# Mamba phase of a four-block network: each scan step cut into two halves, the next chunk's preparation placed by half steps, mean square and row scaling on ScalarE, and GpSimd's product released by the next step's scan

## The reference, cut to what matters

```
n      = rmsnorm(x) * norm_w
xb, z  = split(n @ in_w.T)
xb     = silu(causal_conv(xb, 4 taps) + cb)
dt, B, C = split(xb @ xp_w.T)                  # 16 + 16 + 16
delta  = softplus(dt @ dtw.T + dtb)
dA     = exp(delta[..., None] * -exp(a_log))
mi     = delta[..., None] * B * xb[..., None]
v      = 0.6 * v + mi                          # over the tokens
h      = dA * h + v                            # over the tokens
y      = sum_n h[..., n] * C[..., n] + dp * xb
x      = x + (y * silu(z)) @ out_w.T
```

## Time and profile before

| | |
|---|---|
| median of 3 runs | 5011.13 us |
| lowest, highest | 5005.98, 5019.97 us |
| the profiled execution's own time | 5015.33 us |
| its span | 5013.6 us |
| mean granted clock of TensorE | 0.856 of full speed |
| busy share PE, DVE, ACT, POOL | 74%, 61%, 39%, 41% |

### The profile page before, as it was taken

The page is one execution under the profiler, slowest core; times in us unless marked ns, Lnnn a source line. Parts: engine busy times, 40 slices in busy tenths (PEclk is TensorE's granted clock), DMA queues, the critical chain, the costliest instruction groups (busy, mean ns, idle before and its releaser), DMA issues. The chain is left out here.

```text
span 5013.6 us, 95420 instructions
## 1 busy us (share of the span) xinstructions
PE 3692.2 (74%) x29740; PEld 2429.9 (48%) x29741; DVE 3059.5 (61%) x5150; ACT 1968.5 (39%) x4502; POOL 2051.2 (41%) x1225
## 2 busy tenths in 40 slices
PE   6888879368878878888567888878787431888870
PEld 3555556245545555455345555455554231666660
DVE  3444423457787877878557777877787651333334
ACT  1121112155555655556255555555555120323320
POOL 1011000145565656656445665656556505000006
PEclk8887879779988999899779889989999755999995
DMA  1000000112121221212121121211212152000003
GB/s 44 0 0 0 0 18 0 50 36 67 44 68 45 54 59 46 66 45 64 37 52 52 45 68 45 65 46 47 67 45 67 59 200 83 30 29 30 30 24 100
DMA packets 156167, 241.78 MB, mean 48 GB/s; under 512 B 26450, under 2 KB 84082, under 8 KB 153076
## 3 DMA queue, kind: packets, MB, share of 16 engines
q1 hardware_dynamic: 146164, 210.61, 14.9%
q0 software_dynamic: 9600, 26.23, 1.6%
HBM read 118.86 MB, written 36.18 MB: 31 GB/s over the span
## 5 line engine op out<-in xcount | busy, mean ns | idle before, releaser
L870 POOL TENSOR_TENSOR m_hc<-m_h,m_Cb 128x1024 f32<-128x1024 f32 x512 | 1216.9, 2380 | 1061.5 <-PE m_bank L1244 534.6
L998 DVE TENSOR_TENSOR_SCAN m_h<-m_dA,m_hlast,m_bank 128x256 f32<-128x256 f32 x2048 | 1338.4, 724 | 174.1 <-PE m_bank L1262 167.8
L1244 PE MATMUL m_bank<-m_hc,ident 128*128 128x512 f32 x2048 | 1166.9, 698 | 42.4 <-POOL m_hc L870 37.4
L1260 PE MATMUL m_bank<-m_M,m_U 128*128 128x64 bf16 x8192 | 650.1, 199 | 461.4 <-DVE m_h L998 279.0
L1260 PEld LDWEIGHTS m_bank<-m_M,m_U 128*128 128x128 bf16 x8192 | 585.0, 102 | 679.8 <-DVE m_h L998 486.3
L1115 ACT ACTIVATE m_dA<-m_delta,m_rate 128x256 f32<-128x256 f32 x2048 | 872.1, 503 | 38.2 <-DVE m_h L998 34.7
L1262 PE MATMUL m_bank<-m_M,m_U 112*128 112x64 bf16 x8192 | 649.2, 199 | 0.0
L1262 PEld LDWEIGHTS m_bank<-m_M,m_U 112*128 112x128 bf16 x8192 | 582.6, 102 | 69.6 <-issue 61.7
L1244 PEld LDWEIGHTS m_bank<-m_hc,ident 128*128 128x128 f32 x2048 | 397.7, 216 | 357.3 <-issue 301.1
L947 DVE SCALAR_TENSOR_TENSOR m_cv<-m_xpre,m_conv,m_cv 128x256 f32<-128x256 f32 x384 | 312.9, 856 | 19.5 <-ACT m_cv L1054 15.0
L1121 ACT COPY m_hlast<-m_h 128x4 f32<-128x4 f32 x512 | 97.9, 191 | 507.2 <-DVE m_h L998 506.8
(11 more groups left out here) (264 smaller groups left out, 5975.0 us busy)
## 6 DMA issues: line engine op xcount, KB each, us to landing
m_Cb<-m_c_rows SPq DMA_DIRECT2D x256, 256.0 KB, 3.2
m_M<-m_Mhi SPq DMA_DIRECT2D x128, 256.0 KB, 4.5
m_M<-m_Mlo SPq DMA_DIRECT2D x64, 256.0 KB, 4.9
m_U<-m_Uhi SPq DMA_DIRECT2D x128, 128.0 KB, 2.9
g_stage<-in_e_w SPq DMA_DIRECT2D x16, 1024.0 KB, 6.9
slots_x<-x_res SPq DMA_DIRECT2D x36, 256.0 KB, 6.3
x_x_in<-slots_x SPq DMA_DIRECT2D x72, 128.0 KB, 2.0
slots_y<-x_y POOLq DMA_DIRECT2D x72, 128.0 KB, 2.0
```

Source lines behind the costliest of these rows:

```text
L870: nc.gpsimd.tensor_tensor(hc[:, n % 2], h[:, n % RING], Cb[:, g % 2, n % NG, :].unsqueeze(1).broadcast_to([P, KI, CM]), ALU.mult).then_inc ...
L998: nc.vector.tensor_tensor_scan(h[:, n % RING, m, :], dA[:, n % RING, m, :], VB[(n % 2) * 2 + m // 2][:, (m % 2) * CM:(m % 2 + 1) * CM], hl ...
L1244: last = nc.tensor.matmul(Y[half][:], net.ident[:], hc[:, n % 2, 2 * half:2 * half + 2, :], start=(n == 0), stop=(n == NS - 1))
L1260: nc.tensor.matmul(bank[:, at:at + SUB], U1[:, par, j, m * P:(m + 1) * P], M1[:, par, j, n, :], start=True, stop=False)
```

## The change

`OFF` becomes 8 and counts half steps; the index `at` of a head now runs over half steps, so a chunk's step n has the halves 2n and 2n + 1, and the head of chunk c+1 has index half + 8. Velocity, accumulate, decays and scan are cut in two: each half g takes the channel groups 2g and 2g + 1. The order on PE within a half is velocity g, accumulate g, then the pieces.

The pieces move to these head indices (local half steps in brackets; those from 24 on are in the chunk before): squares 0 (24) and root 1 (25), row scaling 3 (27), transposes 4 (28), xT 5 (29), halo 6 (30), in_proj one tile at each of 6 to 13 (30, 31, 0 to 5), ACT's copies 8 and 10 (0, 2), convolution 11 and 13 (3, 5), silu 15 (7), x_proj 16 (8), B rows 18 (10), dt projection 20 (12), Gf and first Mf 20, second Mf 22, first Mlo 24 (16), second Mlo and Glo 26 (18), series 25 (17), softplus end 27 (19), u 28 (20), transposes of u 30 (22), Uhi 31 (23), Ulo 32 (24), carry matmuls 33 (25), chi 34 (26), clo 35 (27). The tail: gate at half 4, POOL's multiplication at half 6, out_proj at 9 and 10 (now into H1), addition to x at 11. x_proj and the B rows now use H0.

The statistics on DVE (bn_stats, bn_aggr and two small tensor_tensors) are replaced by two ACTIVATEs of Square with an accumulator on ACT, and the row scaling is done by two ACTIVATEs on ACT. `product` waits for one more scan: the first quarter of the next step's. On POOL the product of step 15 moves to step 0 of the next chunk. On SP, place_m now stands ahead of spread 6.

The core of the diff:

```diff
-RING, LEAD, OFF, NG = 4, 2, 5, 2
+RING, LEAD, OFF, NG = 4, 2, 8, 2
...
-                    for g in (4, 5, 6):
+                    for g in (4, 5):
                         spread(c, par, g)
                     if not last:
                         place_m(c + 1, 1 - par)
+                    spread(c, par, 6)
+                    if not last:
                         place_u(c + 1, 1 - par)
...
-                    if at == 15:
-                        matrix_low(q, 1)
-
-                def tail(t, par, slot):
-                    if slot == 2:
+                def tail(t, par, at):
+                    if at == 6:
                         pool.wait_ge(s["gate_done"], 1 + t * KI + KI)
...
-                def product(c, par, n):
+                def product(c, par, n, next_scan=1):
                     k = c * NS + n
                     g = n // NG
-                    pool.wait_ge(s["scan_done"], 1 + AHEAD + (k + 1) * KI)
+                    pool.wait_ge(s["scan_done"], 1 + AHEAD + (k + 1) * KI + next_scan)
                     pool.wait_ge(s["acc_done"], 1 + AHEAD + k - 1)
...
+                    tiles = [xm[:, (q + 1) * TM + j, :] for j in range(TM)]
+                    if at == 0:
+                        for j in range(TM):
+                            nc.scalar.activation(xr[:, j, :], tiles[j], ACT.Square, accum_out=ssq[:, j:j + 1]
+                                                 ).then_inc(s["rms_in"], 1)
+                    if at == 3:
+                        act.wait_ge(s["rms_out"], 1 + q + 1)
+                        act.sem_inc(net.carrier, 1)
+                        for j in range(TM):
+                            nc.scalar.activation(xr[:, j, :], tiles[j], ACT.Copy, scale=rstd[:, j:j + 1]
+                                                 ).then_inc(s["xr_done"], 1)
...
                 def slots(c, par, more, more2):
                     for n in range(NS):
-                        if n < NS - 1:
-                            velocity(c, par, n + 1)
-                        elif more:
-                            velocity(c + 1, 1 - par, 0)
-                        if n >= 2:
-                            accumulate(c, n - 2)
-                        else:
-                            late(c, n)
-                        tail(c, 1 - par, n, more)
-                        if more:
-                            head(c + 1, 1 - par, n + OFF)
-                        if more2 and n + OFF >= NS:
-                            head(c + 2, par, n + OFF - NS)
...
+                        for at in (2 * n, 2 * n + 1):
+                            g = at % 2
+                            if n < NS - 1:
+                                velocity(c, par, n + 1, g)
+                            elif more:
+                                velocity(c + 1, 1 - par, 0, g)
+                            if n < 2:
+                                late(c, n, g)
+                            elif n > 2:
+                                accumulate(c, n - 2, g)
+                            elif g == 1:
+                                accumulate(c, 0, 0)
+                                accumulate(c, 0, 1)
+                            tail(c, 1 - par, at, more)
+                            if more:
+                                head(c + 1, 1 - par, at + OFF)
+                            if more2 and at + OFF >= 2 * NS:
+                                head(c + 2, par, at + OFF - 2 * NS)
```

More of the change, by code:

```diff
@@ L928, in head @@
                 def head(q, par, at):
[L929 to L942, removed]
+                    if at in (11, 13):
+                        g = (at - 11) // 2
                         dve.wait_ge(s["pre_done"], 1 + q * 2 + g + 1)
-                        dve.wait_ge(s["halo_done"], 1 + q + 1)
                         for k in range(TAPS - 1):
@@ L1238, in accumulate, with tail @@
-                def accumulate(c, n):
+                def tail(t, par, at, more):
+                    if at in (9, 10):
+                        j = at - 9
+                        if j == 0:
+                            pe.wait_ge(s["gated_done"], 1 + t + 1)
+                            pe.wait_ge(s["xm_done"], 1 + t)
+                            if more:
+                                pe.wait_ge(s["z_done"], 1 + (t + 1) * 2 + 2)
+                        for k in range(KI):
+                            last = nc.tensor.matmul(H1[:, j * D:(j + 1) * D], u[:, k, j * P:(j + 1) * P],
+                                                    w_out[:, k, :], start=(k == 0), stop=(k == KI - 1))
+                        if j == TM - 1:
+                            last.then_inc(s["out_psum"], 1)
@@ L1239, in accumulate @@
+                def accumulate(c, n, half):
                     k = c * NS + n
-                    pe.wait_ge(s["hc_done"], 1 + AHEAD + k + 1)
+                    if half == 0:
+                        pe.wait_ge(s["hc_done"], 1 + AHEAD + k + 1)
                     if n == 0:
-                        pe.wait_ge(s["gate_done"], 1 + c * KI + KI)
-                    for half in range(2):
-                        last = nc.tensor.matmul(Y[half][:], net.ident[:], hc[:, n % 2, 2 * half:2 * half + 2, :],
-                                                start=(n == 0), stop=(n == NS - 1))
@@ L1246, in accumulate, with velocity @@
-                    last.then_inc(s["acc_done"], 1)
-                def velocity(c, par, n):
+                        pe.wait_ge(s["gate_done"], 1 + c * KI + 2 * half + 2)
+                    last = nc.tensor.matmul(Y[half][:], net.ident[:], hc[:, n % 2, 2 * half:2 * half + 2, :],
+                                            start=(n == 0), stop=(n == NS - 1))
+                    if half == 1:
+                        last.then_inc(s["acc_done"], 1)
+                def velocity(c, par, n, g):
@@ new lines, in velocity @@
+                    bank = VB[(n % 2) * 2 + g]
+                    for m in (2 * g, 2 * g + 1):
+                        for j in range(NSUB):
+                            at = (m % 2) * CM + j * SUB
+                            nc.tensor.matmul(bank[:, at:at + SUB], U1[:, par, j, m * P:(m + 1) * P],
+                                             M1[:, par, j, n, :], start=True, stop=False)
+                            last = nc.tensor.matmul(bank[:, at:at + SUB], U2[:, par, j, m * P:(m + 1) * P],
+                                                    M2[:, par, j, n, :], start=False, stop=True)
@@ L1266, in slots, with late @@
+                    last.then_inc(s["v_psum"], 1)
+                def late(c, n, half):
+                    if not (isinstance(c, int) and c == 0):
+                        accumulate(c - 1, n + NS - 2, half)
                 def slots(c, par, more, more2):
                     for n in range(NS):
-                        if n < NS - 1:
-                            velocity(c, par, n + 1)
-                        elif more:
-                            velocity(c + 1, 1 - par, 0)
-                        if n >= 2:
-                            accumulate(c, n - 2)
-                        else:
-                            late(c, n)
@@ L1287, in _ @@
+                for at in range(2 * NS + OFF):
                     head(0, 0, at)
```

270 lines of the change are left out of this document (133 added, 137 removed).

## The result

The changed kernel takes 4887.3 us (median of four executions, 4877.3 to 4896.9) against 5014.0 for the kernel before in the same session: 0.9748 of it, interval 0.9724 to 0.9773, which is 127 us less. The direction and the range of the prediction held; its size did not, since 54 us were forecast. The profiled execution took 4885.9 us, with a span of 4884.2.

The account below looks back on a forecast made before the run. Waits, not a full engine, bound the kernel: a chain forecast at 44.4 + 25.4 + 3.8 + 12.9 = 86.5 us per period against 88.3. 30 x 1.8 = 54 us less gives 4961, by the median 4957; range 4865 to 5080.

Parts of the forecast that it names:

- The chain: One period of the Mamba loop, velocity 0 to velocity 0, as pieces A, B, C: 86.5 us forecast against 88.3.
- The sum is 88.3.: Present period of one chunk: pieces of 44.15, 25.4 and 18.7 us, cut at velocity 0 at 2033.73 and 2122.05.
- Product 5 starts at 44.4: End of the stretch from velocity 0 to GpSimd's product 5, forecast at 44.4 us; 44.15 before.
- piece A: From velocity 0 to GpSimd's product 5, with TensorE and VectorE handing over: 44.15 us before, 44.4 forecast.
- I take 25.4 again: GpSimd's twelve instructions from product 5, reordered with two lock waits kept: 25.4 us, so u ends at 69.8.
- piece B: GpSimd's nearly packed stretch of twelve instructions from product 5: 25.4 us before and in the forecast.
- u to transposes, Uhi and Ulo takes 3.8 us: Start of piece C: from u's end at 69.8 to Ulo done at 73.6, 3.8 us.
- the last piece: Piece C, SP's DMAs and the carries up to the next velocity 0: 18.7 us before, 3.8 + 12.9 forecast.
- The prologue and the last chunk of a layer keep their order: zero.: Edges outside the 30 periods, forecast to change by zero.
- Occupancy pays in full: Rival: VectorE's relief shows in full, at least 4.5 us per period, 135 us in all: 4875; chance 0.18.
- Release is no release: Rival: a later scan changes nothing for GpSimd's product; period within 0.5 us of 88.3, 5011 within 15; chance 0.14.
- One lock wait too many: Rival, pieces A and B: each whole-product wait of 2.35 us lengthens the period; one gives 5027, two 5098; chance 0.28.

Follow-up runs that it names:

- e2_rms: The kernel before, with only the mean square and the row scaling moved to ScalarE: 5001.1 us, 0.9974 of the kernel before.
- e3_both: The kernel before, with second Mlo ahead of u, M's DMAs ahead of spread 6, and mean square and rows on ScalarE: 4927.3 us, 0.9831 of it.
- e9_whole_gate5: The changed kernel with TensorE's velocity and accumulate in whole steps and GpSimd's gate multiplication ahead of product 2: 4686.4 us, 0.9331 of the kernel before.
- e4_norel: The changed kernel with the product released by its own scan again, as before: 4870.0 us, 0.9720 of the kernel before.
- e6_whole: The changed kernel with TensorE issuing both halves of velocity and accumulate at a step's first half, other engines keeping halves: 4794.9 us, 0.9576 of the kernel before.
- e1_order: The kernel before, with only the second Mlo moved ahead of u and M's DMAs ahead of spread 6: 4934.0 us, 0.9839 of the kernel before.
- e7_gate5: The changed kernel with GpSimd's gate multiplication one half step earlier, ahead of product 2: 4803.9 us, 0.9578 of the kernel before.

## Why the prediction was right and wrong

**The chain was right.** Counted from velocity 0 at 1987.11, forecast against this period: gate multiplication starts 25.9 against 25.3; xb ends 31.8 against 31.1; x_proj 3.45 against 3.53; product 5 starts 44.4 against 43.4; u ends 69.8 against 68.35; Ulo ends 73.6 against 71.1; carries issued 78.6 to 79.3 against 77.15; velocity 0 again 86.5 against 84.6. Of the signs that the text named, these are there: U's DMAs behind u (2.8 us, some 4 forecast), M issued at product 9, z not before 28 us (29.06), x_proj's idle time (4.60) and its lower clock. Three are not as named: the period is 84.6 and not 86 to 87, TensorE's wait for the carries is still there but 2.7 us a time and not 4 to 5, and a convolution instruction takes 624 ns in the mean and not below 600.

**The size was missed by several terms, nearly all to one side.** The steps that failed:
- "The sum is 88.3." The base period came from one pair of velocity 0. Eleven periods in the middle of a layer give 88.74 in the mean. 30 x 0.44 is 13 us. (From clo to clo all 30 periods have a mean of 88.29, since the first and the last of a layer are shorter; those became shorter in the changed kernel too, so middle periods are to be compared with middle periods.)
- "Product 5 starts at 44.4", piece A: 43.4, and about 41.7 in the periods in which TensorE does not show its lower level behind velocity 0. Thirteen periods of the changed kernel give 84.9 in the mean, with 82.7 to 87.6 between single ones.
- "I take 25.4 again", piece B: 24.95. As foreseen, the lock waits changed place and stayed two: products of 3.33 and 3.35 us instead of the long Mf and Mlo.
- "u to transposes, Uhi and Ulo takes 3.8 us": 2.77. The 3.8 came from a place where an accumulate stood in the way: it ran to 2100.26, 1.37 us past the end of u. In the last piece Ulo to clo took 6.0 us against the 4.9 (by clo) or 5.7 (by the queue) of the forecast, and clo to velocity 0 7.47 against some 7.9; the two together are 13.47, which is 0.57 more than the 12.9 of the sum and goes against the other three.
- "The prologue and the last chunk of a layer keep their order: zero." The edges changed too. From clo to clo, the 15 periods of the first layer lost 55.6 us and those of the second 60.0; the stretch between the layers lost 7.7 (170.0 to 162.3), and that before the first clo 2.7. So 10 us lay in a term that I had set at zero without a row.

Together: a period 1.6 us shorter than forecast is 48, the base 13, the edges 10, and with the 54 forecast that makes 125 of the 127. Counted directly, the 30 periods lost 115.6 us from clo to clo, 3.85 each, where 1.8 each was forecast. No one of the terms is large; the forecast was short by more than half because its own gain, 1.8 of 88.3 us, was a small difference of large terms.

**The costs set at nothing.** Mean square and rows were costed at zero. Done alone they are worth 15 us at most (e2_rms) and 7 beside the order (e3_both): right. The accumulating form that no row showed takes 0.41 and, as an instruction of its own, 0.20 us more:

```profile
2058.10 0.41 ACT L1046 ACTIVATE m_pair<-x_res 128x256 f32 x1
2058.40 0.20 ACT L1046 ACTIVATION_READ_ACCUMULATOR m_pair<-x_res 128x1 f32 x1
```

Half a microsecond was forecast for each, so this term held.

**The rivals.** "Occupancy pays in full" gave 4875 and came within 12 us of the time, by another road: e2_rms took the tiny instructions off VectorE in the kernel before and got 15 us, not 135, although VectorE's busy time fell by 219. The 135 was itself too high a price: it took 2.27 us for L934 as for L935, but L934 has a mean of 1.68, and the two lines fill 117.9 us of the span together. The Trainium skill, "Perfetto Trace Analysis", section Identifying the Most-Contended Engine, would have the busiest engine relieved first; here VectorE lost 11 us of busy time in a period, and the period followed by 4, while e9_whole_gate5 took some 200 us more off with VectorE busier than in the changed kernel (2814.3 us against 2722.9). "Release is no release" was right of the release and wrong of the whole: e4_norel moves nothing that can be told. "One lock wait too many" did not come, but the reason named for it, halves behind each other on TensorE, is what e6_whole shows to cost 86 us.

**What I did not see.** In the text the halves on TensorE were only a row of terms of piece A. I never asked what the same chain would be with whole steps on TensorE. Nor did I follow up that the gate multiplication is "free to start at 19" but stands behind product 2, and ask what that place alone was worth: 85 us. And I credited the second Mlo's move with M's DMAs only; that it frees VectorE's tiny instructions from the lock (192.4 to 29.5 us in e1_order, together with SP's line) I had put down to the work going to ScalarE.

**Left open.** Why single periods differ by up to 5 us is not settled; they go mostly with TensorE's level behind velocity 0, but nothing here moves that alone. The 0.0255, some 130 us, between e3_both and e6_whole were not divided among the placements of the single pieces. The moves of Mlo and of SP's line were tried together and SP's line alone, never Mlo's place alone. Which engine makes the piece between product 5 and u 3.1 us longer when TensorE's steps are whole and the release is early was not taken apart.

## What to carry to other kernels

Before an engine is relieved of work, ask whether its instructions are long in themselves or by what stands beside them: one instruction of GpSimd moved by two steps, with one line of SP's, took 163 us of busy time off VectorE. On an engine that runs in order, ask of a finer cut whether one half comes to stand behind a wait that the whole did not have; here it paid to leave TensorE whole and to keep the halves on the engines behind it. A release that does nothing in one order may be worth 161 us in another, so test it again after each change of the order.

## What was not expected of the hardware

- **The lock costs both sides.** The Trainium skill, "SBUF — State Buffer", section SBUF: two separate sides, says that whichever of a GpSimd instruction that reads SBUF and a VectorE instruction with two SBUF inputs starts first holds the shared ports for its whole length. The trace agrees to some 0.15 us: L957 runs from 2039.41 to 2040.76, so 1.13 us of it are left when GpSimd starts its product at 2039.63, and that product takes 3.33 us instead of 2.35, a surplus of 0.98.
- **A wait on TensorE can be paid twice.** The same eight matmuls take 1.93 us at a granted clock of 1.00 (2.4 GHz) and 3.53 at 0.53, near the lower level of 1.2 GHz, after 4.60 us of idle time. The idle time right before does not settle it alone: after 3.74 us of it x_proj takes 1.93 to 3.65 us in single periods of e6_whole, and with none right before it 1.93 to 3.65 in those of e7_gate5.
- **DMAs of one size do not take one time to issue.** SP needs 0.67 us for each of the first three DMAs of M and 1.16 to 1.35 for the three behind them (2.70 for two at 2052.58), while those of U, which are half as large, take 0.6 each but for the last (1.55). What sets this no run shows.
